# Attention in eight paired steps a head, with block transposes on VectorE and a DRAM scratch in place of TensorE transposes

## The reference

```python
xn = layernorm(x)                               # x: 2048 tokens x 256
k, q, v = (einsum('ihd,bpd->biph', W, xn) for W in (W_K, W_Q, W_V))   # 16 heads of 128
scores = einsum('biph,biqh->biqp', k, q)        # causal mask
attn = softmax(masked / sqrt(128), axis=-1)
z = einsum('biqp,biph->biqh', attn, v)
attn_out = einsum('df,bqf->bqd', W_O, z_flat)
ffn = einsum('bsh,dh->bsd', fwht(silu(xn @ W1.T) * (xn @ W3.T)), W2)  # hidden 1024
out = x + attn_out + ffn
```

## Time and profile before

| | us |
|---|---|
| median of 2 runs | 1658.88 |
| the runs | 1656.48 and 1661.29 |
| span of the profiled execution | 1653.5 |
| TensorE, VectorE, ScalarE, GpSimd busy in it | 1590.5, 1088.2, 958.8, 261.4 |

### The profile page before, as it was taken

One profiled execution on the slowest core, in us unless ns is written; L12 is line 12 of the kernel. 1 busy time (PEld: TensorE's weight loads), 2 busy tenths in 40 slices (PEclk: granted clock), 3 DMA queues, 4 the chain that ended last, 5 costly groups with the idle time before them and its releaser, 6 DMA issues.

```text
span 1653.5 us, 31426 instructions
## 1 busy us (share of the span) xinstructions
PE 1590.5 (96%) x10536; PEld 1428.3 (86%) x10536; DVE 1088.2 (66%) x2776; ACT 958.8 (58%) x2071; POOL 261.4 (16%) x209
## 2 busy tenths in 40 slices
PE   4999999999999999999999999999999999999998
PEld 3888898998989898988989898989989898989987
DVE  6433675858667675858677675758576676758585
ACT  3322474756657574746567474747566574747565
POOL 4200111212121211112021202112021212112111
PEclk7999999999999999999999999999999999999999
DMA  3000000000000000000000000000000000000000
GB/s 129 26 1 0 1 1 14 0 0 13 0 13 0 13 0 13 0 1 13 0 13 0 13 0 13 0 13 0 0 13 0 13 0 13 0 13 0 0 20 33
DMA packets 7259, 16.65 MB, mean 10 GB/s; under 512 B 512, under 2 KB 4736, under 8 KB 6784
## 3 DMA queue, kind: packets, MB, share of 16 engines
q1 hardware_dynamic: 7168, 15.80, 2.9%
HBM read 13.70 MB, written 2.10 MB: 10 GB/s over the span
## 4 chain that ended last, share of the span: by engine, by line
PE 91%; issue 4%; DVE 2%; ACT 2%; DMA 1%; DVEq 0%; SPq 0%; POOL 0%; POOLq 0%
PE ps L738 25%; PE ps L740 25%; PE ps L739 25%; PE ps L864 14%; PE ps L879 2%; DMA probs<-w1t 1%; ACT q_hi L421 1%; DVE z_lo L673 0%; DVE w_raw L520 0%; DVE ps L637 0%; ACT probs L446 0%; DVE pt_lo L555 0%; DVE neg_max L648 0%; DVE stats L534 0%; ACT pt_hi L381 0%
## 5 line engine op out<-in xcount | busy, mean ns | idle before, releaser
L428 ACT CAST pt_hi<-ps 128x512 fp32r<-128x512 f32 (+3 forms) x640 | 320.5, 525 | 237.0 <-PE ps L864 230.5
L655 DVE TENSOR_TENSOR pt_lo<-ps,pt_hi 128x512 fp32r<-128x512 f32 (+3 forms) x640 | 369.4, 606 | 41.5 <-ACT pt_hi L428 34.2
L446 ACT ACTIVATE probs<-ps,neg_max 128x1024 f32<-128x1024 f32 (+9 forms) x384 | 332.8, 871 | 89.2 <-DVE neg_max L648 84.8
L642 DVE TENSOR_REDUCE bank_max<-ps 128x1 f32<-128x512 f32 x384 | 264.7, 689 | 139.0 <-PE ps L740 137.0
L864 PE MATMUL ps<-ident,probs 128*128 128x128 f32 x2176 | 321.9, 274 | 30.3 <-ACT probs L446 30.2
L738 PE MATMUL ps<-pt_hi,v_hi 128*128 128x256 f32 (+1 forms) x1152 | 339.2, 294 | 2.6 <-DVE z_lo L673 2.6
L331 POOL TENSOR_TENSOR acc<-w_a,acc 128x512 f32<-128x512 f32 x128 | 164.3, 1284 | 1106.3 <-ACT w_a L462 1106.3
L740 PE MATMUL ps<-pt_hi,v_lo 128*128 128x256 f32 (+1 forms) x1152 | 324.5, 282 | 0.0
L739 PE MATMUL ps<-pt_lo,v_hi 128*128 128x256 f32 (+1 forms) x1152 | 324.5, 282 | 0.0
L864 PEld LDWEIGHTS ps<-ident,probs 128*128 128x128 f32 x2176 | 256.5, 140 | 71.0 <-issue 33.5
L738 PE MATMUL ps<-k_hi,q_hi 128*128 128x512 f32 (+3 forms) x640 | 251.5, 393 | 0.0
(11 more groups left out here) (95 smaller groups left out, 2215.8 us busy)
## 6 DMA issues: line engine op xcount, KB each, us to landing
w_raw<-w_heads SPq DMA_DIRECT2D x16, 512.0 KB, 3.3
acc<-x SPq DMA_DIRECT2D x4, 512.0 KB, 11.4
out<-acc SPq DMA_DIRECT2D x8, 256.0 KB, 2.1
w_a<-w2t SPq DMA_DIRECT2D x1, 1024.0 KB, 8.2
probs<-w1t SPq DMA_DIRECT2D x1, 1024.0 KB, 11.2
probs<-w3t SPq DMA_DIRECT2D x1, 1024.0 KB, 13.2
w_b<-hadamard SPq DMA_DIRECT2D x1, 64.0 KB, 3.2
```

Source lines behind the costliest of these rows:

```text
L428: act.copy(pt_hi4[:, (j // 2) % 2, 4 * g:4 * g + n, (j % 2) * P:(j % 2 + 1) * P], bank(ring_bank((j, g)), 0, n * P).rearrange("p (t q) -> ...
L446: act.activation(probs[:, j % 2, b * BANK:b * BANK + n], ps[:, at:at + n], ACT.Exp, bias=neg_max[:, j:j + 1], accum_out=row_part[:, j, e:e ...
L642: dve.tensor_reduce(bank_max[:, j, b:b + 1], ps[:, at:at + n], AX_X, ALU.max).then_inc(maxed, 1)
L655: dve.tensor_tensor(pt_lo4[where], bank(ring_bank((j, g)), 0, n * P).rearrange("p (t q) -> p t q", q=P), pt_hi4[where].bitcast(F32), ALU.s ...
```

## The change

**Steps.** A head now has eight steps. Step s takes row 15-s (the large one, 4 or 3 banks) and row s (the small one, 1 or 2 banks): 17 tiles and five banks in every step, with banks 0 to 4 held by scores and no second buffer. There are three exponentials a step; the scores of a step wait for the exponential of the step before on the same banks. Banks 5 and 6 are a ring of two for all projections and outputs, bank 7 stays for the weighted sums.

**Transposes.** ScalarE writes the exponentials as blocks into `raw` (two buffers). VectorE transposes each 32x32 block in place, one instruction a row. SP stores the row to a DRAM scratch, waits until it has landed, and brings it back with four loads, each onto 32 partitions, so that whole tiles come out transposed in `pt_lo`. ScalarE copies that to `pt_hi`, and GpSimd subtracts in place for `pt_lo`. V goes the same way, with four stores a quarter in pieces of 32 elements and one load.

**Order.** Stores of step s and loads of step s stand in SP's queue in steps s and s+1, splits in s+2, the weighted sum of a pair of rows from two steps later on, partly in the next head. Projections for the next head are spread over steps 4 to 7 and the steps 0 and 2 of that head. SP's program is written out for all heads and has three weight loads a head.

**At the start**, the copy of the Hadamard product and the mask come later, since buffers are shared in another way; the first projections wait until the FFN is added.

Core of the diff (new functions and what they replace):

```diff
-    SCORE_BANKS = 4
-    RING = 3
+    STEP_BANKS = 5
+    def big_banks(s):
+        return 4 if s < 4 else 3
+    def row_of(s, small):
+        return s if small else TILES - 1 - s
+    def exps_of(s):
+        n = big_banks(s)
+        return [(0, 2), (2, n), (n, STEP_BANKS)]
+    Z_ORDER = [7, 0, 6, 1, 5, 2, 4, 3]
+    Z_BIG = {0: (-1, 4), 1: (-1, 4), 2: (-1, 6), 3: (-1, 6), 4: (0, 0), 5: (0, 0), 6: (0, 2), 7: (0, 2)}
+    Z_SMALL = {1: (-1, 5), 3: (-1, 7), 5: (0, 1), 7: (0, 3)}
+    RING = 2
...
+        scratch = [nc.dram_tensor(f"scratch{j}", [P, (j + 1) * P], F32).ap() for j in range(TILES)]
+        v_scratch = [nc.dram_tensor(f"v_scratch{b}", [BLK, 4 * BANK], F32).ap() for b in range(QUARTERS)]
...
+            def send(h, s, small):
+                sp.wait_ge(blocked, 2 * (STEPS * h + s) + small + 1)
+                sp.dma_start(scratch[row_of(s, small)], raw_row(s, small)).then_inc(stored[small], 16)
+            def bring(h, s, small):
...
+                wait(sp, moved[small], 64 * (STEPS * h + s))
+                sp.wait_ge(stored[small], 16 * (STEPS * h + s + 1))
+                back = scratch[j].rearrange("(a k) (g x) -> g k a x", a=4, g=4)
+                for g in range(4):
+                    to = pt_row(pt_lo, j)[g * BLK:(g + 1) * BLK].bitcast(F32).rearrange("k a i q -> k a (i q)")
+                    sp.dma_start(to, back[g]).then_inc(moved[small], 16)
+            def send_v(h, b):
+                sp.wait_ge(v_blocked, v_count(h, b))
+                to = v_scratch[b].rearrange("k (b a d) -> a k b d", a=4, d=BLK)
+                for a in range(4):
+                    sp.dma_start(to[a], v_raw[a * BLK:(a + 1) * BLK, :].rearrange("k (b d) -> k b d", d=BLK)
+                                 ).then_inc(v_stored, 16)
...
+                sp.dma_start(v_lo[:, b * BANK:(b + 1) * BANK].bitcast(F32),
+                             v_scratch[b].rearrange("k (g x) -> g k x", g=4)).then_inc(v_moved, 16)
+            for h in range(HEADS):
+                for s in range(STEPS):
...
+                    hh, ss = step_before(h, s, 1)
+                    if hh >= 0:
+                        bring(hh, ss, 0)
+                        bring(hh, ss, 1)
+                    if s == 1:
+                        bring_v(h, 3)
+                    send(h, s, 0)
+                    send(h, s, 1)
+                    if s < 4:
+                        send_v(h, V_ITEMS[s])
...
+            def p_to_lo(h, s, n):
...
+                pool.wait_ge(pt_hi_done, piece_count(h, s, n))
+                pool.tensor_tensor(lo, lo.bitcast(F32), hi.bitcast(F32), ALU.subtract).then_inc(pt_lo_done, 1)
...
-                    act.copy(pt_hi4[:, (j // 2) % 2, 4 * g:4 * g + n, (j % 2) * P:(j % 2 + 1) * P],
-                             bank(ring_bank((j, g)), 0, n * P).rearrange("p (t q) -> p t q", q=P)
-                             ).then_inc(ring_hi, 1)
+                act.wait_ge(moved[n == 2], 64 * (STEPS * h + s + 1))
+                act.copy(pt_row(pt_hi, j, a, b), pt_row(pt_lo, j, a, b).bitcast(F32)).then_inc(pt_hi_done, 1)
...
+                to = raw_row(s, small).rearrange("p (g i k) -> p i g k", g=4, k=BLK)
+                act.activation(to[:, first // P:(first + n) // P],
+                               ps[:, a * BANK:a * BANK + n].rearrange("p (i g k) -> p i g k", g=4, k=BLK), ACT.Exp,
+                               bias=neg_max[:, j:j + 1], accum_out=row_part[:, j, e % 2:e % 2 + 1]
+                               ).then_inc(exped, 1)
...
+            def transpose_blocks(h, s, small):
+                dve.wait_ge(exped, piece_count(h, s, 2 if small else 1))
+                v = raw_row(s, small).rearrange("p (b k) -> p b k", k=BLK)
+                dve.transpose(v, v).then_inc(blocked, 1)
...
-                    for i in range(4 * g, min(4 * g + 4, j + 1)):
-                        ins = pe.transpose(bank(ring_bank((j, g)), (i % 4) * P, (i % 4 + 1) * P),
-                                           probs[:, j % 2, i * P:(i + 1) * P], ident[:, :])
-                    ins.then_inc(ring_filled, 1)
+                    p = [pt_chunk(t, c)[:, lo:8, i, :] for t in (pt_hi, pt_lo)]
+                    ins = mm3(bank(Z, lo * BLK, CHUNK_Q), v, p, n == 0, n == len(tiles) - 1)
```

More of the change, by code:

```diff
@@ L87, in attention_ffn_kernel @@
[L87 to L102, removed]
@@ L253, in _ @@
             sp.wait_ge(xn_transposed, TILES // 2)
[L254 to L262, removed]
+            sp.dma_start(w_raw[:, 0:2, :], w_heads[0][:, 0:2, :]).then_inc(qk_loaded, 16)
@@ L353, in _ @@
+            with pool.Fori(1, HEADS - 1) as h:
+                period(h)
+            period(HEADS - 1, more=False)
+            period(HEADS, over=True)
         @block.scalar
@@ L512, in _ @@
+            act.activation(table_use[:, 2:3], ones[:, :], ACT.Exp)
+            for item in KQ_ITEMS[2:]:
+                kq_to_hi(-1, item)
+            period(0, first=True)
+            with act.Fori(1, HEADS - 1) as h:
+                period(h)
+            period(HEADS - 1, more=False)
+            period(HEADS, over=True)
         @block.vector
@@ L723, in head @@
[L723 to L731 removed]
+                        dve.tensor_reduce(bank_max[:, j, i:i + 1], scores, AX_X, ALU.max).then_inc(maxed, 1)
+                dve.wait_ge(maxed, 4 * (STEPS * h + s) + (4 if small else len(parts)))
@@ L734, in _ @@
+            dve.wait_ge(mask_ready, 2)
+            for item in KQ_ITEMS[2:]:
+                kq_to_lo(-1, item)
+            period(0, first=True)
+            with dve.Fori(1, HEADS - 1) as h:
+                period(h)
+            period(HEADS - 1, more=False)
+            period(HEADS, over=True)
         @block.tensor
@@ new lines, in project_v, with scores @@
+            def project_v(h, b):
+                ring_wait(h, ("V", b))
+                if b == 3:
+                    pe.wait_ge(wv_split, h + 1)
+                project_slice(bank(ring_bank(("V", b))), 2, slice(b * BANK, (b + 1) * BANK)
+                              ).then_inc(v_projected, 1)
+            def scores(h, s):
+                hh, ss = step_before(h, s, 1)
+                for pos in range(STEP_BANKS):
+                    small = pos >= big_banks(s)
+                    b = pos - (big_banks(s) if small else 0)
+                    j = row_of(s, small)
+                    if pos == 0 or exp_of(ss, pos) != exp_of(ss, pos - 1):
+                        wait(pe, exped, piece_count(hh, ss, exp_of(ss, pos)) if not first_step(h, s) else 0)
+                    if s == 0 and pos < 3:
+                        pe.wait_ge(proj_lo, kq_count(h - 1, ("K", pos)))
+                    if s == 4 and pos == 0:
+                        pe.wait_ge(proj_lo, kq_count(h, ("Q", 1)))
@@ L971 @@
+            pe.wait_ge(hidden_done, HT * QUARTERS + G_FREE)
+            pe.wait_ge(ffn_added, PER_Q * QUARTERS + 1)
+            for item in KQ_ITEMS[2:]:
+                project_kq(-1, item)
+            period(0, first=True)
+            with pe.Fori(1, HEADS - 1) as h:
+                period(h)
+            period(HEADS - 1, more=False)
+            period(HEADS, over=True)
 def kernel(L0_attn_x, L0_attn_W_K, L0_attn_W_Q, L0_attn_W_V, L0_attn_W_O, L0_ffn_W1, L0_ffn_W2, L0_ffn_W3):
```

858 lines of the change are left out of this document (442 added, 416 removed).

## The result

The changed kernel takes **1828.38 us** (1823.06 to 1833.69, 2 runs) against 1658.88: a ratio of 1.104, 95% interval 1.099 to 1.108. It is slower by a tenth; 1536 us and "faster" had been forecast, and the range ended at 1700. A second time, beside the kernel before at 1655.13, it took 1818.3, ratio 1.099 [1.095, 1.102].

What follows compares the result with a forecast made beforehand. TensorE was taken to bound the kernel before; after the change, transfers set steps 0 to 3 and TensorE the others. 178 + 9 + 16 x 82.4 + 25 = 1530.4, plus 5.4, gave 1536 us; range 1395 to 1700.

Steps and rivals of the forecast that it cites:

- What the engines cost: Busy time per head: TensorE 71.7 us, VectorE 64.2, ScalarE 64.2, GpSimd 61.8, so TensorE the busiest engine.
- contention of the earlier trace: GpSimd's subtractions: one row took 4.42 us, not 2.35, while VectorE worked on SBUF; +36 a head if all did.
- signs for a wrong forecast: Block transpose far from 2.3 us; large-row load over 1.5 with head over 90; TensorE over 95%, head 74; strided matmuls above 0.12.
- signs named for a right forecast: No TensorE transposes; head 80 to 84 us; DMA share 0.8 or more; waits on exponentials or GpSimd's lo; longer steps 0 to 3.
- The term for b: Loads of probabilities from DRAM per step: 1.11 MB taken at 4.7 us, between 3.4 at 330 GB/s and 6.8.
- The rival of half-rate loads: Probability loads onto 32 partitions at half rate, b = 6.8: head 97 us, 1769 us; chance only within "slower", 0.18.
- V loads and weights 0.7: Transfers in steps 0 to 3: V's loads and the weight loads together put at 0.7 us a step.
- V stores 3.2: Transfers in steps 0 to 3: V's 2,048 packets of 128 B at 25 ns, 3.2 us; bounds 0.6 to 6.4.
- A V step: Each of steps 0 to 3: 2.8 + 3.2 + 4.7 + 0.7 = 11.4 us, set by the transfers.
- Steps 4 to 7 at 9.2: Steps without V: transfers need 8.65 us, less than 9.2, so TensorE sets them.
- TensorE's pace without V: TensorE's pace with its transposes gone: 9.2 us a step, 73.8 a head, the most that can be won.
- waits at before's rate: TensorE's waits per head kept at 4%, as in the kernel before, on 71.7 us of work.

Runs made afterwards that it cites:

- without V's trip: Changed kernel without V's stores to and loads from DRAM; V's halves made from the block buffer, values wrong: 1551.7 us, ratio 0.937.
- with stores only: Changed kernel with V's stores kept, its loads left out and V's halves made from the block buffer: 1570.0 us.
- unread loads: Changed kernel without V's stores, V's loads landing in a bank nothing reads: 1685.0 us with loads on 4 engines, 1557.9 with loads on 16.
- direct V: Changed kernel with V projected keys-on-partitions, without transpose, store or load of V, and steps, ring order and lo-half engine rearranged: 1574.4 us, ratio 0.950.

## Why the prediction was wrong

*Right, by its steps.* What the engines cost. The block transpose, an operation without a row, was put at 2.3 us for 2,048 elements; GpSimd at 2.35 for 1,024 and 1.28 for 512, with the contention of the earlier trace rows taken at nothing:

```profile
L760 DVE STREAM_TRANSPOSE raw<-raw 128x2048 f32<-128x2048 f32 x16 | 37.0, 2311 | 26.8 <-ACT raw L536 26.8
...
L381 POOL TENSOR_TENSOR pt_lo<-pt_lo,pt_hi 128x1024 fp32r<-128x1024 f32 x48 | 113.2, 2372 | 205.9 <-ACT pt_hi L545 205.9
L386 POOL TENSOR_TENSOR v_lo<-v_lo,v_hi 128x512 fp32r<-128x512 f32 x64 | 81.6, 1275 | 201.1 <-ACT v_hi L522 201.1
```

The moving operand in runs of 32 keeps its 0.12 us from start to start (740.33, 740.45 and 740.57 in a row of weighted sums without V's trip). The head without V's trip keeps all the work of these engines and has VectorE busy for 57.1 us, ScalarE 54.7 and GpSimd 61.3, where 64.2, 64.2 and 61.8 had been worked out. None of them paces. Of the signs for a wrong forecast, a head of over 90 came, but not the loads it was tied to: 256 KB at 218 GB/s take 1.2 us, not over 1.5. Of the signs named for a right forecast some came: a DMA share of 0.79 in the head shown above, longer steps 0 to 3, SP waiting for its stores. TensorE's waits, though, were named wrongly: they stand on V's lo half, not on that of P.

*The term for b* was low by an eighth. Loads onto 32 partitions run at 201 to 223 GB/s in the windows of a head, so 1.11 MB takes 5.3 us, not 4.7. The Trainium skill (SBUF — State Buffer, Door 1: The DMA port swizzle) gives a ceiling of about 218 for this; the trace agrees within a few per cent. The rival of half-rate loads (b = 6.8, 1769 us) is not what happened, though its time is not far from the measured one: b was 5.3, and loads onto all 128 partitions brought 40 us with V's trip and 4 without.

*The step that failed first* is "V loads and weights 0.7", and with it "V stores 3.2", read as sums of bytes. A V step was priced at 11.4 in place of 9.2, 8.8 us a head in all; V's trip costs 17.3. The load was priced at full rate on all engines, though its access pattern has four outer blocks, and it was never asked whose turn it takes: SP holds everything behind it. Its small stores, feared at up to 6.4 us, are worth 41 us of 1828 by removal. Missing altogether are what turns V's trip from bytes into delay: SP's wait between two V loads, one block buffer that stays taken until its stores have landed (146.4 us of ScalarE's waits), and the date. The price of the buffer is open: no run gave a second one, and with stores only ScalarE still waits 102.5 us for them, while all of the stores cost 18. No run left out SP's wait between the V loads or projected V earlier either. V is projected in steps 0 to 3 and needed in 4; store, landing, load, hi and lo in a row did not fit, and TensorE stands 10.7 us a head. "Steps 4 to 7 at 9.2" was the sentence in which that wait belonged. The runs put lateness at 68 to 78 us and traffic at 199.

*The second step that failed* is TensorE's pace without V, 73.6 (8 x 9.2, "waits at before's rate"). The sum itself was a little low: 4% on 71.7 gives 74.6, not 73.8. The kernel without the trip has a head of 787.30 - 704.45 = 82.9:

```profile
704.40:787.30 82.90, 75.89 (x458) 66.58 (x457) 57.11 (x129) 54.74 (x113) 61.33 (x43) 0.98 0.82 221
```

TensorE is idle for 7.0 us of it. Its largest wait there is the one for ScalarE's copy of an output before a projection may use its bank: 75.4 us in 30 times, 4.7 a head, and 75.3 in the changed kernel. The prediction looked for a loss only at the exponentials. The rest of the gap, some 5 us a head, is smaller waits, a granted clock of 0.98 and what the busy times overlap; no run split it.

The two terms add up. V's trip: 17.3 - 8.8 = 8.5 a head. The rest: 82.9 - 73.6 = 9.3. Together 17.8 x 16 = 285 us, where 292 were missing. The first alone (1536 + 136 = 1672) would have lost the forecast's gain, and the second alone (1536 + 149 = 1685) as well.

*The clock* is part of both and in neither term. The mean granted clock is 0.897 in the changed kernel, 0.958 without V's trip, and 0.993 before, where it was 1.00 in an attention window. It is at 0.50 behind the long stop of TensorE. So a wait of 10.7 us costs more than itself. An estimate from the rows above: over 746 to 756 TensorE is busy for 4.21 us, all of it at half its full clock, and loses about 2 us by that. No run measured it by itself.

## What to carry to other kernels

Price a transfer by its place before its bytes: which DMA engines its access pattern reaches, what stands behind it in the same in-order queue, when its buffer comes free, and how many steps lie between its first producer and its first reader. Look at the outermost dimension of both sides of every load; V's 64 unread loads, each with four outer blocks, cost 127 us more than four loads of one block each in their place, for the same bytes. And where a transpose is wanted only because of a projection's orientation, turn the projection round: direct V, with its new order, made a slowdown of 10% into a gain of 5%.

## What the runs showed of the hardware

- A load with 4 outer blocks ran at 77 GB/s at a DMA share of 0.25, two with 2 blocks each at 35 GB/s and 0.14, while stores in the same queue reached 408 GB/s at 1.01.
- SP is held 0.46 us by the issue of a load of probabilities (eight in 3.65) and 0.97 by that of a store of V in 512 packets of 128 B (four in 3.88). The count of packets explains little of it: the same four stores with 32 packets of 2 KB each took 3.47, a load of 128 KB of weights behind the stores of a step 0.97, and the first load of x, with 512 packets of 1 KB, 0.44. What sets the time stays open.
- A block transpose on VectorE costs 2,311 ns for 2,048 elements of four bytes and 691 for 512, the slope of its other operations.
- Loads onto 32 partitions of SBUF ran at 201 to 223 GB/s. With neighbours in the queue going to different groups of partitions (0, 2, 1, 3), the kernel took 1571.2 us against 1574.4, which says little, since TensorE is busy for 93% there; the queue's share fell from 70.0% to 66.5% for the same bytes, so the loads themselves may have gained a few per cent.
